# Transposes placed between the bf16 products of an expert tile

## The reference

```python
x = x + tanh(g_xattn) * xattn(layernorm(x), ctx, ctx, Wq, Wk, Wv)
...
scores = softmax(xf @ Wg.T)                 # xf = layernorm(x), 8 experts
expert_weights, expert_indices = top_k(scores, 2)
h1 = xf @ W1.T + (xf @ A1.T) @ B1.T + b1     # per expert, 256 -> 512
h3 = xf @ W3.T + (xf @ A3.T) @ B3.T + b3
g = silu(h1) * h3
y_e = g @ W2.T + (g @ A2.T) @ B2.T + b2      # 512 -> 256
x = x + tanh(g_ffn) * sum over the two experts of weight * y_e
```

## Time and profile before

| | before |
|---|---|
| runs on the chip | 330.58, 328.56, 330.31 us; median 330.31 us |
| the profiled execution, first to last instruction (span) | 325.4 us |
| median of the runs less that span | 4.9 us |
| busy share of the span | PE 92%, PEld 71%, DVE 76%, ACT 63%, POOL 65% |

### The profile page before, as it was taken

How to read it: one execution, slowest core, us unless ns; L and a number is a source line. 1 busy time by engine, 2 the same in 40 slices (tenths; PEclk the granted TensorE clock), 3 DMA queues, 4 the chain that set the end, 5 groups by cost and what they waited for, 6 DMA issues and landing times. The chain is left out here.

```text
span 325.4 us, 7435 instructions
## 1 busy us (share of the span) xinstructions
PE 297.9 (92%) x1755; PEld 230.0 (71%) x1755; DVE 248.2 (76%) x607; ACT 206.0 (63%) x486; POOL 210.8 (65%) x246
## 2 busy tenths in 40 slices
PE   7589989999997798999999999999999999999960
PEld 3468778788886656776777777777777777777740
DVE  2679879889999998697988976767776776777750
ACT  5635755766878577787675565665675665675550
POOL 2457878888893098866756656766577776666241
PEclk9799999999999699999999999999999999999996
DMA  7968997999972169567747675766533223333100
GB/s 265 391 158 240 280 297 253 294 279 278 278 244 85 17 225 296 138 201 200 205 139 206 175 187 186 175 187 197 148 56 55 52 51 66 53 45 61 20 0 0
DMA packets 30424, 54.35 MB, mean 167 GB/s; under 512 B 7232, under 2 KB 15808, under 8 KB 30112
## 3 DMA queue, kind: packets, MB, share of 16 engines
q1 hardware_dynamic: 14672, 36.10, 34.1%
q0 software_dynamic: 7488, 9.36, 16.7%
q10 hardware_dynamic: 8224, 8.42, 8.6%
HBM read 41.92 MB, written 10.65 MB: 162 GB/s over the span
## 5 line engine op out<-in xcount | busy, mean ns | idle before, releaser
L1079 POOL DMA_INDIRECT out<-ys,cols x39 | 64.7, 1660 | 58.4 <-DMA out<-ys,cols 33.0
L883 ACT ACTIVATE gh<-bank 128x512 fp32r<-128x512 f32 x39 | 23.4, 599 | 61.0 <-PE bank L648 61.0
L640 PE MATMUL bank<-WH,xh 128*128 x156 | 55.7, 438 | 0.1
L1056 POOL DMA_INDIRECT xg<-xn_rows,colg x39 | 40.0, 1026 | 20.5 <-POOL colg L1034 10.3
L992 POOL TENSOR_TENSOR WL<-stage,WH 128x512 bf16<-128x512 f32 x38 | 47.9, 1278 | 7.3 <-ACT WH L752 7.1
L640 PE MATMUL bank<-WH,xl 128*128 x156 | 49.0, 395 | 0.0
L640 PE MATMUL bank<-WL,xb 128*128 x156 | 47.2, 385 | 0.0
L752 ACT ACTIVATE WH<-stage 128x512 fp32r<-128x512 f32 x38 | 22.9, 628 | 17.7 <-DVE stage L1110 14.5
L640 PEld LDWEIGHTS bank<-WH,xl 128*128 128x128 f32 x156 | 29.2, 188 | 6.8 <-DVE xl L1493 0.4
L1497 DVE TENSOR_TENSOR gl<-bank,gh 128x512 fp32r<-128x512 f32 x39 | 26.9, 689 | 8.8 <-ACT gh L883 8.7
L657 PE MATMUL bank<-WH,gh 128*128 x156 | 32.0, 327 | 1.5 <-ACT gh L883 1.5
(11 more groups left out here) (229 smaller groups left out, 702.2 us busy)
## 6 DMA issues: line engine op xcount, KB each, us to landing
BB<-biases_in SPq DMA_DIRECT2D x16, 640.0 KB, 4.1
stage<-w_all_in SPq DMA_DIRECT2D x38, 256.0 KB, 5.1
BA<-biases_in SPq DMA_DIRECT2D x8, 640.0 KB, 3.9
WL<-w_all_in SPq DMA_DIRECT2D x10, 256.0 KB, 4.7
LS<-WH SPq DMA_DIRECT2D x45, 48.0 KB
xn_rows<-xn ACTq DMA_DIRECT2D x8, 256.0 KB, 4.1
out<-x ACTq DMA_DIRECT2D x7, 256.0 KB, 3.1
cx<-ctxT_in ACTq DMA_DIRECT2D x6, 256.0 KB, 6.5
```

Source lines behind the costliest of these rows:

```text
L640: last = nc.tensor.matmul(dst[:, :], lhs[p][:, c * P:(c + 1) * P], W[:, bass.ds(e * (UNITS * UC) + (2 * kind + c) * UC, HID)], start=(part ...
L883: nc.scalar.activation(gh[:], pG[:, :], ACT.Copy).then_inc(s_gh, 1)
L1056: nc.gpsimd.indirect_dma_start(out=xg[q][:], out_offset=None, in_=xn2_d[0:JA * P, :] if i < NA else xn2_d, in_offset=bass.IndirectOffsetOn ...
L1079: nc.gpsimd.indirect_dma_start(out=out_rows, out_offset=bass.IndirectOffsetOnAxis(ap=cols[:, i:i + 1], axis=0), in_=ys[p][:], in_offset=No ...
```

## The change

Only the tile loop is touched. The six transposes of a tile no longer stand in a row. Each stands in front of one product with bf16 weights: the four of g (tile i-1) in front of the `xb` products of h1 and h3 of tile i, the two of x in front of the first two `gb` products of y. For that, h3 begins with its `xb` products, and y takes `gb` second and `gl` last. From tile 5 on, the x of a tile is transposed one step sooner, inside y of tile i-1 in step i for tile i+2 (`ahead`); tiles 1 to 4 keep their step (`i < AHEAD`). ACT and DVE take the parts of x before those of g in those steps.

```diff
+AHEAD = 4
...
+            def y_tile(i, e, ahead):
+
+                pos_wait(pe, s_ys, i)
+                pe.wait_ge(s_gh, i + 1)
                 for c in range(HC):
-                    last = nc.tensor.transpose(pG[:, c * P:(c + 1) * P], g[:, c * P:(c + 1) * P], ident[:])
-                last.then_inc(s_gT, 1)
...
+                    down(e, gh, WH, c, start=(c == 0))
+                if ahead:
+                    x_free(ahead)
+                pe.wait_ge(s_gb, i + 1)
+                for c in range(HC):
+                    if ahead and c < CH:
+                        x_last = x_transpose(ahead, c)
+                        if c == CH - 1:
+                            x_last.then_inc(s_xT, 1)
+                    down(e, gb, WL, c)
+                pe.wait_ge(s_gl, i + 1)
+                for c in range(HC):
+                    last = down(e, gl, WH, c, stop=(c == HC - 1))
                 last.then_inc(s_y, 1)
...
             def tile(i, q, first, more):
                 p = q % 2
-                up(pH1, i, p, expert(q), 0, s_h1)
...
+                pe.wait_ge(s_xb, i + 1)
                 if not first:
-                    g_transposes(i - 1)
-                if more:
-                    x_transposes(i + 1, (q + 1) % XBUF)
+                    pe.wait_ge(s_g, i)
+                for c in range(CH):
+                    if not first:
+                        g_transpose(c)
+                    last = up(pH1, p, e, 0, xb, WL, c, stop=(c == CH - 1))
+                last.then_inc(s_h1, 1)
                 if first:
                     pe.wait_ge(s_wl, (E - 2) * UNITS + 4)
-                up(pH3, i, p, expert(q), 1, s_h3)
+                pos_wait(pe, s_h3b, i)
+                for c in range(CH):
+                    if not first:
+                        g_last = g_transpose(CH + c)
+                        if c == CH - 1:
+                            g_last.then_inc(s_gT, 1)
+                    up(pH3, p, e, 1, xb, WL, c, start=(c == 0))
+                if i < AHEAD:
+                    x_transposes(i + 1, (i + 1) % XBUF)
+                for c in range(CH):
+                    up(pH3, p, e, 1, xh, WH, c)
+                for c in range(CH):
+                    last = up(pH3, p, e, 1, xl, WH, c, stop=(c == CH - 1))
+                last.then_inc(s_h3, 1)
...
-                    down(i - 1, expert((q - 1) % XBUF))
+                    y_tile(i - 1, expert((q - 1) % XBUF), i + 2 if AHEAD - 1 <= i < NT_SLOTS - 2 else 0)
```

On ACT and on DVE:

```diff
+                if more and i >= AHEAD:
+                    x_parts(i + 1, 1 - p)
                 if not first:
                     g_high(i - 1)
-                if more:
+                if i < AHEAD:
                     x_parts(i + 1, 1 - p)
...
                 biased(h1, pH1, i, x, 0, s_h1, s_h1b)
+                if more and i >= AHEAD:
+                    x_rest(i + 1, 1 - p)
                 if not first:
                     g_rest(i - 1)
-                if more:
+                if i < AHEAD:
                     x_rest(i + 1, 1 - p)
```

More of the change, by code:

```diff
@@ L631, in x_transposes @@
                 last.then_inc(s_xT, 1)
[L633 to L643, removed]
@@ L645, in g_transposes, with up @@
-            def g_transposes(i):
-                pe.wait_ge(s_g, i + 1)
-                for c in range(HC):
-                    last = nc.tensor.transpose(pG[:, c * P:(c + 1) * P], g[:, c * P:(c + 1) * P], ident[:])
-                last.then_inc(s_gT, 1)
[L651 to L659, removed]
+            def up(dst, p, e, kind, lhs, W, c, start=False, stop=False):
+                return nc.tensor.matmul(dst[:, :], lhs[p][:, c * P:(c + 1) * P],
+                                        W[:, bass.ds(e * (UNITS * UC) + (2 * kind + c) * UC, HID)], start=start, stop=stop)
@@ new lines, in g_transpose, with down, x_free @@
+            def g_transpose(c):
+                return nc.tensor.transpose(pG[:, c * P:(c + 1) * P], g[:, c * P:(c + 1) * P], ident[:])
+            def down(e, lhs, W, c, start=False, stop=False):
+                return nc.tensor.matmul(pY[:, 0:D], lhs[:, c * P:(c + 1) * P],
+                                        W[:, bass.ds(e * (UNITS * UC) + 4 * UC + c * D, D)], start=start, stop=stop)
+            def x_free(i):
+                pe.wait_ge(s_xg[i % XBUF], 16 * (i // XBUF + 1))
+                pe.wait_ge(s_xh, i)
+                pe.wait_ge(s_xb, i)
+                pe.wait_ge(s_xl, i)
@@ new lines, in x_transpose @@
+            def x_transpose(i, c):
+                return nc.tensor.transpose(pX[:, c * P:(c + 1) * P], xg[i % XBUF][:, c * P:(c + 1) * P], ident[:])
+            def y_tile(i, e, ahead):
+                pos_wait(pe, s_ys, i)
+                pe.wait_ge(s_gh, i + 1)
+                for c in range(HC):
+                    down(e, gh, WH, c, start=(c == 0))
[11 more added lines that the diff above has]
+                    last = down(e, gl, WH, c, stop=(c == HC - 1))
@@ L674, in tile @@
                 p = q % 2
-                up(pH1, i, p, expert(q), 0, s_h1)
-                if not first:
-                    g_transposes(i - 1)
-                if more:
-                    x_transposes(i + 1, (q + 1) % XBUF)
+                e = expert(q)
+                pos_wait(pe, s_h1b, i)
+                pe.wait_ge(s_xh, i + 1)
+                for c in range(CH):
+                    up(pH1, p, e, 0, xh, WH, c, start=(c == 0))
+                pe.wait_ge(s_xl, i + 1)
+                for c in range(CH):
+                    up(pH1, p, e, 0, xl, WH, c)
+                pe.wait_ge(s_xb, i + 1)
+                if not first:
+                    pe.wait_ge(s_g, i)
[4 more added lines that the diff above has]
+                last.then_inc(s_h1, 1)
                 if first:
                     pe.wait_ge(s_wl, (E - 2) * UNITS + 4)
-                up(pH3, i, p, expert(q), 1, s_h3)
+                pos_wait(pe, s_h3b, i)
[7 more added lines that the diff above has]
+                    x_transposes(i + 1, (i + 1) % XBUF)
+                for c in range(CH):
+                    up(pH3, p, e, 1, xh, WH, c)
+                for c in range(CH):
+                    last = up(pH3, p, e, 1, xl, WH, c, stop=(c == CH - 1))
+                last.then_inc(s_h3, 1)
                 if more:
@@ L718, in _ @@
             tile_steps(pe, tile)
-            g_transposes(NT_SLOTS - 1)
-            down(NT_SLOTS - 1, expert((NT_SLOTS - 1) % XBUF))
+            pe.wait_ge(s_g, NT_SLOTS)
+            for c in range(HC):
+                last_gT = g_transpose(c)
+            last_gT.then_inc(s_gT, 1)
+            y_tile(NT_SLOTS - 1, expert((NT_SLOTS - 1) % XBUF), 0)
         @block.scalar
```

## The result

| | before | after |
|---|---|---|
| median of the runs, us | 330.44 (4 runs, 328.56 to 331.51) | 334.41 (4 runs, 333.24 to 338.9) |
| ratio to before, 95% interval | | 1.0116 [1.0069, 1.0163] |
| span of the profiled execution, us | 325.4 | 332.7 |

After is slower by 1.2%, clear of noise; the forecast was 334.8 us. The two medians lie 4.0 us apart and the two spans 7.3. Every execution on record with both numbers has 1.8 or 1.9 us outside its span, so the profiled one of before took some 327.2 us, less than any of its four runs; that of after (334.5 us) lies at the median.

What follows compares the result with a forecast made beforehand. PE alone was taken to bound the loop, 4.82 us a tile, with POOL's scatters as busy in one stretch. +2.81 us for the gather wait and +1.73 for the order on PE gave +4.54, 334.8 us; range 328.8 to 338.0.

Steps and rivals of the forecast that it cites:

- the wait for the gathers: PE's transposes of x, asked for 2.94 us sooner, wait for unmoved gathers on POOL: net +2.81 us.
- the order on PE: New neighbours among PE's products and transposes: 23 tiles from 16 on at +0.075 us, +1.73 us.
- The second rival: Gathers on POOL land in time, so x costs less: 330.8 us, no change; chance 0.28.
- Transposes hide nothing: On PE, a transpose is 0.11 us of stream and 0.06 us of load; a bf16 product beside it hides nothing.
- The first rival: On PE, weight loads limit transposes and pairs hide them, 0.31 us a tile: 319.1 or 328.1 us; chance 0.17.
- two cycles a column: On PE, a transpose of 128 f32 columns seems to stream two cycles a column: 273 against 275 ns for 256 bf16 columns.
- The switches behind fp32r: On PE, two transpose loads behind fp32r products exposed at 0.06 us replace three bf16 switches at 0.015: +0.075 us a tile.
- the end of the range not taken, -0.045 us: What a tile's switches on PE change if nothing of the transpose loads behind fp32r products is exposed: -0.045 us.
- `gh`: no wait: In y, `gh` is ready 0.60 us after its start, wanted 1.15 us after the last transpose of g: no wait.
- The sum of a tile, 4.82 us: PE's work in one tile before: 1.38 + 0.44 + 0.22 + 1.38 + 1.40 = 4.82 us.
- `gb`: In y, `gb` starts 0.60 to 1.21 us after `gh`; wait of 0 to 0.2 us a tile, taken as 0.
- the 4.9 us between span and median: Difference between before's profiled span and the median of its runs, taken to stay: 330.31 + 4.5 = 334.8 us.

Runs made afterwards that it cites:

- Kernel 2: The kernel before with only the sooner x: its transposes between `gh` and `gl` of y, parts of x ahead of those of g; 332.40 us, ratio 1.0074.
- kernel 3: After, with POOL issuing each gather one step sooner, from step 3 on; 331.96 us, ratio 1.0058.
- kernel 9: After, with all four transposes of g in h1, two in front of each `xb` product, none in h3; 331.64 us, ratio 1.0015.
- kernel 10: After, with all four transposes of g in h1 and each gather issued one step sooner; 330.17 us, ratio 0.9991.
- Kernels 6 and 7: 6: after with x in its old step and y in its old order, 333.23 us; 7: the same with each transpose of g made twice, 350.50 us.
- kernel 1: After without the sooner x: x transposed in its old step, its parts copied in their old place; 339.71 us, ratio 1.0319.
- kernel 8: Against kernel 1, `gb` made right behind `gh` on ACT, ahead of the copies of x; 342.75 us, ratio 1.0397.
- kernel 11: Against kernel 10, y keeps `gb` last in steps 1 to 3, where x is not yet copied ahead of g; 329.92 us, ratio 0.9994.

## Why the prediction came out

The time was right, 334.8 against 334.41 us, and of the two parts of its sum the first, the wait for the gathers, was right in kind. The second, +1.73 us from the order on PE, was right by luck: one of its terms had the wrong sign, and another, put at nothing, cost 2 to 3 us, more than the whole part.

**The gathers: right in kind, and sized high if anything.** The forecast had x asked for 2.94 us sooner, the gathers not moved, and +2.81 us of waiting. Kernel 2 makes only this part and costs 2.4 us, by its interval 1.0 to 3.9. Its longest wait, 2.4 us, is for the very gather of tile 17 that the forecast chose: tile 15, in whose step it stands, takes 7.41 us against 4.82 before. In after the form differs, ten waits of up to 1.5 us and not one. Taking the waits away wins 0.58% from after to kernel 3 and 0.24% from kernel 9 to 10, 1.9 and 0.8 us, neither clear of noise. The second rival, gathers in time, is excluded by these waits.

**Transposes hide nothing: right.** Kernels 6 and 7 put a transpose's stream at 0.11 us wherever it stands. The first rival falls. The "two cycles a column" of the step was the author's estimate from 273 and 275 ns; no run counts cycles, and what the runs show is the 0.11 us for 128 columns.

**The switches behind fp32r: wrong.** The step took +0.06 us for each of two loads of transposes behind fp32r products, because the plain f32 load of the earlier trace rows had waited there. In after the transpose of g behind `xl` adds 0.11 us (247.56), its bare stream, and in kernel 10 so does the transpose of x behind `gh` (249.91). Nothing is exposed. The idle time that was to show itself ahead of these loads did not come either: over 204 to 310 us the loads of the transposes of g idle 1.7 us in after, against the 4.2 of the earlier trace rows. That is the end of the range not taken, -0.045 us; with `gh` in time, kernel 10 measured 4.78 - 4.84 = -0.06. The trace of before had shown the very case once. Right behind its fp32r products of `LS` (L495) stand four transposes (128.4 to 129.4 us, PE and its loads):

```profile
128.36 0.72 PE L495 MATMUL bank<-LS 128*128 128x256 f32 x4
128.92 0.60 PE L502 MATMUL bank<-ident,xn 128*128 128x128 f32 x4
128.82 0.46 PEld L502 LDWEIGHTS bank<-ident,xn 128*128 128x128 f32 x4
```

The products end at 129.08 and the four transposes at 129.52, which is 4 x 0.11 us, and their first load began at 128.82, 0.26 us before the products ended. This row is nearer than the plain f32 load that the step went by.

**"`gh`: no wait": wrong, and the term that mattered.** The step counted that `gh`, ready 0.60 us after its start, is wanted 1.15 us after the last transpose of g. But in the trace of after a load begins ahead of its product (the first of `xl` at 258.64, its product at 258.87), and the queue's records have an address instruction for each `gh` product ahead of its load. The load could begin 259.06 - 258.39 = 0.67 us after `gh` starts, and not 1.15. In the queue's records the four addresses begin at 259.13, 259.28, 259.41 and 259.53, the first of them 0.14 us after `gh` ends, and each load some 0.1 us behind its own; in kernel 10 the first begins at 253.40, 0.41 us ahead of its load. So `gh` that ends 0.07 us before its load could begin is still 0.19 us late. The price is 4.90 - 4.78 = 0.12 us a tile in the mean, and 4.85 - 4.76 = 0.09 between the two tiles shown: `gh` products 0.51 us instead of 0.47, and the next transpose 0.15 instead of 0.11, are the part that the chain shows. Kernels 9 and 10 make the last transpose sooner, and the price goes; that it was the place of the last transpose is shown. From after to kernel 9 the ratio falls from 1.0116 to 1.0015, 3.3 us, with intervals that do not touch, and from kernel 3 to 10 by 0.67%, 2.2 us. So this term weighs as much as the gathers. That the address instructions are what turns a just-in-time semaphore into lost time is read from the queue's records and was not tried by itself.

Together a late tile costs 4.90 - 4.84 = +0.06 us, where +0.075 was taken for another reason: -0.06 from the switches and +0.12 from `gh`. The sum of a tile, 4.82 us, took 1.38 for h1 where the earlier trace rows has 1.42; the late period of 4.84 lies between, and nothing hangs on it.

**`gb`: right, for its reason.** There is no wait for it in after beyond 0.2 us: it starts 259.07 - 258.39 = 0.68 us after `gh`, near the sooner end of the 0.60 to 1.21 that the step gave. What the forecast did not say is how much hangs on it. It treated the sooner x as a cost alone; kernel 1 shows that with the copies of x still in the way `gb` comes late in 36 steps and the kernel is at +10 us, and kernel 8 that another order on ACT only moves the wait to g.

**Left out.** Tiles 1 to 4 keep x's old step while y already takes `gb` second; in the steps of tiles 2 and 3 this adds 0.3 and 0.6 us (after: 6.04 and 5.46 against 5.72 and 4.82). In kernel 11 taking most of it back won no time. And the 4.9 us between span and median were carried over to the kernel after, where they are 1.7: right for the difference of medians, because it was before's profiled execution that was short.

## What to carry to other kernels

Before a load is moved to an earlier place on the engine that bounds the kernel, look at what the queue behind that transfer waits for: if the transfer stays where it is, the lead is paid back as waiting in program order (here ten waits of up to 1.5 us). When a step is pulled apart and spread over later products, ask for each of its consumers when the engine wants the data in its queue, loads and addresses included, and not when the product would stream (here 0.67 us after `gh` starts, not 1.15). When a cost is taken from a neighbouring row, look first whether the old trace has the new pair of neighbours itself, if only once. And where two engines have nearly the same pace (POOL 5.1 us, PE 4.8), a gain on one counts only in the stretch in which the other has slack.

## What was not expected of the hardware

- Behind the fp32r products of `xl` a bf16 product exposed some 0.015 us and a transpose nothing (0.11 us at 247.56). In after the f32 weights of that transpose are loaded from 247.16, 0.40 us before the last `xl` product ends, while in the kernel before the bf16 load in that place idles 0.27 us for each pair of `xb`.
- Data that became ready just in time cost PE more than their lateness: in after `gh` ended 0.07 us before its load could begin, and the load began 0.19 us late; in kernel 6 `gb` was ready 0.27 us before its first load, its products run at full pace (0.11 us each), and the loads after them come 0.2 us late.
